# The bias of a message pass as a matrix product over 128 rows in place of three

## What is computed

```
for l in range(3):
    m = concatenate([x[dst], x[src], edge_features])
    m = relu(layernorm(m @ msg_w1[l] + msg_b1[l]))
    m = relu(layernorm(m @ msg_w2[l] + msg_b2[l]))      # msg_b2 is what the change is about
    agg = segment_sum(m, dst)
    h = concatenate([x, agg])
    x = x + relu(layernorm(h @ upd_w[l] + upd_b[l]))
```

## Time and profile before

| | |
|---|---|
| median of three runs | 11508.31 us (11474.56 to 11514.13) |
| profiled execution | 11528.77 us, span 11527.1 us |
| TensorE products, busy | 7972.0 us, 69% of the span |
| TensorE weight loads, busy | 6715.4 us, 58% |
| VectorE, ScalarE, GpSimd, busy | 6403.6, 6095.8, 7190.2 us |
| mean granted clock of TensorE | 0.772 of 2.4 GHz |

### The profile page before, as it was taken

How to read it: one execution, slowest core, us unless ns; L and a number is a source line. 1 busy time by engine, 2 the same in 40 slices (tenths; PEclk the granted TensorE clock), 3 DMA queues, 4 the chain that set the end, 5 groups by cost and what they waited for, 6 DMA issues and landing times. The chain is left out here.

```text
span 11527.1 us, 371235 instructions
## 1 busy us (share of the span) xinstructions
PE 7972.0 (69%) x122953; PEld 6715.4 (58%) x122953; DVE 6403.6 (56%) x15831; ACT 6095.8 (53%) x15991; POOL 7190.2 (62%) x10039
## 2 busy tenths in 40 slices
PE   5444444554334789988899988997889965446656
PEld 4233333332233678887788877886778854436555
DVE  6333333333455368884488636885368854553665
ACT  1333333333354379994499737995368833332332
POOL 2555555555566468885588657885579955555555
PEclk8555555555566899998999999997999986559666
DMA  5111111111477987776877687776989966558555
GB/s 203 40 41 41 41 41 41 40 40 40 150 236 236 286 267 232 233 232 203 299 229 223 167 326 230 226 228 144 390 287 297 297 248 223 160 140 330 181 179 153
DMA packets 1563466, 2189.53 MB, mean 190 GB/s; under 512 B 503499, under 2 KB 1105372, under 8 KB 1548638
## 3 DMA queue, kind: packets, MB, share of 16 engines
q1 hardware_dynamic: 1240382, 1195.69, 34.0%
q0 software_dynamic: 210528, 491.24, 15.2%
q10 hardware_dynamic: 112320, 499.48, 10.8%
HBM read 1245.73 MB, written 827.61 MB: 180 GB/s over the span
## 5 line engine op out<-in xcount | busy, mean ns | idle before, releaser
L633 POOL DMA_INDIRECT by_src<-sort_rec,slots x1560 | 1513.1, 970 | 1434.1 <-DVE sort_rec L702 818.9
L1309 POOL DMA_INDIRECT NEAR<-spread_f,gather_ids_l x1368 | 1375.4, 1005 | 278.7 <-issue 193.2
L1435 ACT ACTIVATE z_l<-z_l,sizes_l 128x64 f32<-128x64 f32 x5472 | 1376.5, 342 | 0.1
L767 PE MATMUL bank<-hots_t 104*128 104x512 bf16 (+3 forms) x1568 | 624.9, 462 | 831.6 <-ACT junk L594 413.8
L660 DVE TENSOR_TENSOR picked<-bank,hots 128x392 f32<-128x392 f32 x392 | 221.1, 564 | 1695.4 <-remote 1386.8
L607 ACT ACTIVATE hots_t<-bank_bf 104x1024 bf16<-104x1024 bf16 x196 | 200.7, 1024 | 1416.5 <-remote 841.8
L767 PEld LDWEIGHTS bank<-hots_t 104*128 104x128 bf16 x1568 | 209.9, 134 | 1139.1 <-ACT junk L594 465.1
L1519 PE MATMUL bank<-wm_diag,zr_t_l 128*128 128x128 f32 x5472 | 803.3, 290 | 0.1
L594 ACT ACTIVATE junk<-bank,minus_one 128x512 bf16<-128x512 f32 (+2 forms) x1176 | 638.0, 543 | 283.2 <-remote 220.0
L1519 PEld LDWEIGHTS bank<-wm_diag,zr_t_l 128*128 128x128 f32 x5472 | 671.9, 193 | 158.3 <-issue 158.3
L1472 PE MATMUL bank<-m_l,hot_wide_l 128*128 128x64 f32 x5472 | 748.6, 280 | 1.2 <-issue 1.1
(11 more groups left out here) (397 smaller groups left out, 27534.3 us busy)
## 6 DMA issues: line engine op xcount, KB each, us to landing
spread_f<-unit_rows_a ACTq DMA_DIRECT2D x342, 512.0 KB, 5.9
hot_wide_l<-dst_wide SPq DMA_DIRECT2D x456, 256.0 KB
unit_hot_a<-src_hots_t SPq DMA_DIRECT2D x342, 256.0 KB, 4.0
near_of_l<-NEARB SPq DMA_DIRECT2D x1368, 48.0 KB
dst_hots<-NEAR SPq DMA_DIRECT2D x114, 512.0 KB
dst_wide<-hot_wide_l SPq DMA_DIRECT2D x114, 512.0 KB
hot_t_l<-dst_hots_t SPq DMA_DIRECT2D x456, 128.0 KB
NEAR<-dst_hots SPq DMA_DIRECT2D x456, 128.0 KB
```

The costliest lines, as they stand in the source:

```text
L633: pool.indirect_dma_start(out=by_src, out_offset=bass.IndirectOffsetOnAxis(ap=slots[h][:, j:j + 1], axis=0), in_=rec[h][:, j, :], in_offse ...
L767: pe.matmul(to, lhsT=cols[:, t * P:width], rhs=cols[:, 0:width], start=True, stop=False, skip_group_check=True)
L1309: pool.indirect_dma_start(out=far_in[h % WA][:, g * GT:(g + 1) * GT, :].rearrange("p j f -> p (j f)"), out_offset=None, in_=spread_f, in_o ...
L1435: last = act.activation(z[h % WA][:, t, :], z[h % WA][:, t, :], ACT.Relu, scale=sizes[h % WA][:, 2, 0, t:t + 1])
```

## The change

`b2rows` and `ones_b` get 128 rows each. `b2rows` is set to zero on GpSimd in the first block, and the three pieces of the bias are put into its first three rows as before. The bias product runs over all 128 rows. The zero rows add nothing. The number of columns, the bank, the order of the instructions and the waits stay as they were.

```diff
-        b2rows = sb("b2rows", [3, LAYERS, 8 * D], BF16)
-        ones_b = sb("ones_b", [3, P], BF16)
+        b2rows = sb("b2rows", [P, LAYERS, 8 * D], BF16)
+        ones_b = sb("ones_b", [P, P], BF16)
...
                 pool.memset(ones_b[:], 1.0).then_inc(zeroed, 1)
+                pool.memset(b2rows[:], 0.0).then_inc(zeroed, 1)
                 pool.wait_ge(consts_ready, 4)
-                pool.wait_ge(zeroed, 9)
+                pool.wait_ge(zeroed, 10)
...
                             bank = BV[h % 2]
-                            pe.matmul(bank[:], lhsT=ones_b[0:3, :], rhs=b2rows[:, l, :], start=True, stop=False,
+                            pe.matmul(bank[:], lhsT=ones_b[:], rhs=b2rows[:, l, :], start=True, stop=False,
                                       skip_group_check=True)
```

## The result

The kernel after takes 11469.26 us (median of 19 runs, 11425.4 to 11506.59), the kernel before on the same chip 11502.74 us (19 runs). The ratio is 0.9972, 95% interval 0.9962 to 0.9983: 33 us less, where 102 were forecast. The profiled execution has a span of 11453.2 us. Of the rivals the second, "the gain is mostly eaten" with 46 us less, comes nearest in size; what ate the gain is only in part what it names, as the experiments show. The time of 11469.26 us also lies inside the stated range, by less than 1 us, and that is luck: the range ended in the middle of this rival, and the sum behind the forecast did not come true.

A forecast was written before the change was run, and what follows sets the result against it. TensorE was taken to bound passes 1 and 2, with ScalarE's 3.58 us step next, and not pass 0. Gains of 91 us there and 11 in pass 0 sum to 102, giving 11406 us against the median 11508.3; range 11335 to 11470.

The forecast's parts named there:

- the gain is mostly eaten: Rival: engines wait for one another and transfers; 0.10 us a step remains, nothing in pass 0; 46 us less, 11462; chance 0.16.
- TensorE bounds passes 1 and 2, not pass 0.: Message passes: TensorE busy 98 and 99% in passes 1 and 2; in pass 0 idle 0.47 us a step.
- Three losses of 0.30 us at the borders, and all go.: Around the three-row bias product: 0.096 us lost before it, 0.098 in it, 0.102 behind it, a step; TensorE saves these.
- The rival of the unchanged borders: Rival: loads at the bias product's borders are late for another reason; 0 us gained, 11508; chance 0.10.
- With three engines within 0.07 of each other that slack is gone, so I take 0.20 a step and leave 0.04 to unevenness.: Passes 1 and 2: ScalarE's 3.58 us step caps the gain at 0.24; 0.20 taken, 91 us over both.
- Pass 0, 11 us less.: Pass 0: TensorE's idle time covers most of the saving; 0.05 us a step taken, of 0.30 possible.
- The other edits.: Start of kernel: new memset at most 1.39 us, larger ones_b tenths, hidden while GpSimd is idle; no wait added in passes.
- Slower by the clock.: Rival: idle TensorE falls to 1.2 GHz, 1.5 us more a step; with 150 such steps +123 us, 11631; chance 0.04.

The follow-up runs named there:

- h4: Kernel after with wide sum products first, window ids loaded once per two steps, seven of eight relu operations, first gather issued once per buffer: ratio 0.9786.
- f5: Kernel before (bias product over three rows), with the wide products of the segment sums ahead of the wait for GpSimd's second message piece: ratio 0.9974.
- e2: Kernel after with seven of ScalarE's eight relu pieces a step, one tile in eight left without: ratio 0.9975.
- f3: Kernel after, with TensorE's wide products of the segment sums ahead of the wait for GpSimd's second piece, 11.5 ms chip: ratio 0.9902.
- k2: Kernel after with the wide products of the segment sums ahead of the wait for GpSimd's second piece, run on a 10.1 ms chip: ratio 0.9913.
- k3: Kernel after with wide products ahead of the wait for the piece and window ids loaded once in two steps, 10.1 ms chip: ratio 0.9871.
- f8: Kernel after with wide products ahead of the wait for the piece and window ids loaded once in two steps, 10.1 ms chip: ratio 0.9873.
- k1: Kernel after, unchanged, run again on a 10.1 ms chip: ratio 0.9948 to the kernel before.
- e4: Kernel after with the sync engine loading window ids once in two steps, nothing else changed, 11.5 ms chip: ratio 0.9978.
- e5: Kernel after with the bias product over 64 of the 128 rows, one run, 11.5 ms chip: passes 1118.8, 887.0, 891.1 us.
- e6: Kernel after with the bias product over 65 of the 128 rows, one run, 10.1 ms chip: passes 1060.1, 854.6, 848.2 us.
- f2: Kernel after with GpSimd making the second message piece before issuing the second gather, 11.5 ms chip: ratio 0.9988.
- f4: Kernel before (bias product over three rows) with GpSimd making the second message piece before the second gather, 11.5 ms chip: ratio 1.0047.

## Why the prediction was wrong, step by step

- **TensorE bounds passes 1 and 2, not pass 0.** Right.
- **Three losses of 0.30 us at the borders, and all go.** Right, each to 0.01 us, and shown by h4 against f5 and by 64 rows against 65. The rival of the unchanged borders fell. The Trainium skill's rule of the drain (TensorEngine Tiling, Key Properties) agrees with all of it: 0.30 us a step where the count of rows changes, none where it doesn't. Its list of configurations, which counts a row tiling from 64 rows down (the Trainium skill, TensorEngine Tiling, Available Configurations), agrees with the step between 65 and 64. The Trainium skill's rule that a load overlaps only when the row groups differ (TensorE: Matmul & The Clock Gate) would have given no gain; the loads that lie ahead of their products after the change speak against it.
- **"With three engines within 0.07 of each other that slack is gone, so I take 0.20 a step and leave 0.04 to unevenness."** This step failed, on both counts. The mean step came to 3.81 and 3.83 us, 0.29 to 0.31 above TensorE's own 3.52, where the step before less 0.20 would be 3.74 and 3.71, and the gain was 49 us in place of 91. TensorE lost 87 of its 136 us again, where the forecast allowed for 45. Of these 87 us 59 stand at the sums: the gaps in the middle of their groups grew by 38.5 us over both passes, and the waits ahead of them by 20, with TensorE right behind GpSimd's piece in 88 steps of 215 where it had been 5 (pass 1). The prediction has no term for either; that the piece was only 1.21 us early in the median step was to be read in the trace of before. The list of engines also left out the sync engine, which issues five transfers and a load of ids in each step. In this run it was busy with that for 3.73 us a step but not late; on the 10.1 ms chips, at 3.68, it is the gate. ScalarE's 3.58 was not the limit: e2 took one of its eight relu operations away, and nothing moved.
- **Pass 0, 11 us less.** Wrong in sign by a little, 10 us more in the profiled executions. Its idle time stood at the sums behind GpSimd's piece, in 207 of 215 steps, and there the saving went. f3 shows it: the edit at that place alone gives 91 us. With wide first in both kernels the bias product is worth 6 us in pass 0 (1037.6 in f5, 1031.3 in k2, two chips of one sort), so taking little was right, and so was the reason, TensorE's idle time.
- **The other edits.** Hidden, as said. **Slower by the clock.** Did not occur, 0.99 in all passes.

So the edit takes 0.30 us a step, 68 us a pass, out of TensorE's own work; that is what it is worth where TensorE stays the bound. On the 11.5 ms chip 28.8 and 20.1 came through. With the wide products first the same edit took 35.7 and 30.4 us off passes 1 and 2 (f5 to k2, same time of the kernel before to 1.2 us), with the ids in pairs as well 56.4 and 55.2 (f5 to k3). k3, and f8, which is the same kernel, are the fastest that compute everything: 0.9871 (0.9854 to 0.9887) for k3, against 0.9948 for the kernel after on that chip.

Shown: the losses, the border between 65 and 64 rows, the piece in pass 0, the sync engine's issues in passes 1 and 2 on the 10.1 ms chips, and where the missing time stands on the chip of the result. Open: what makes the pauses in the sums on the 11.5 ms chips, and so the cause of the larger part of what is missing there. They stand in step with GpSimd's gather, but no run took the gather away on such a chip, and f8's two reliefs together weren't run on one either.

## What to carry to other kernels

Before the gain of a faster bound engine is priced, list for each queue, the one that only issues transfers too, its own step when it waits for nothing, and for each handover into the bound engine how early it arrives in the median step and in the tightest ones. A mean of 0.1 us above the floor says little of what it will be when the floor is lower. When a relief shows nothing, it may have been tried beside a second limit: on one chip wide first alone took 4 us off passes 1 and 2 (k1 to k2), and ids in pairs on top of it 45 (k2 to k3). Compare such versions on the same chip; e4 and f3 against f8 can't tell, since passes 1 and 2 of the unchanged kernel already differ by 33 us between their chips. Put the work that needs the late piece last in its group.

## What the runs showed of the hardware

- A product over 64 rows between products over 128 costs 0.30 us of TensorE at the upper clock level, one over 65 less than 0.01: 96 to 105 ns each at its entry, at its exit and at the first load behind it (e5 and e6).
- The sync engine needs 3.57 us in the median step and 3.68 in the mean to issue five transfers with their window ids (k2, pass 1); with half the loads of ids it waited 61 us in a pass of 828 (k3) in place of 14 in 849.
- The wide transfer of 256 KB lands 3.3 us after its issue in k1 and k2 (median of pass 1).
- Moving one GpSimd operation ahead of a gather's issue (f2, f4) lengthened passes 1 and 2 by 38 to 51 us each although it made the piece early.
- The kernel after has 50 and 47 pauses in passes 1 and 2 on one sort of chip and 1 and 3 on the other (k1), the one with the wide products first 31 and 34 against 1 and 2 (f3, k2), with the same busy times of GpSimd and ScalarE within 1% (f3 and k2, pass 1: 715.5 and 715.9 us, 820.3 and 824.6).
